# Last stage of a four-layer kernel: all steps turn keys and queries first, and the output rows' product and sum are split around the energies and the masking

## What is computed

```python
# third layer, per head; x is normalized first
q, k, v = silu(x @ Wq), silu(x @ Wk), x @ Wv      # q and k are then multiplied by cos and sin tables
energy = einsum('bhnd,bhmd->bhnm', q, k) * tril
out = einsum('bhnm,bhmd->bhnd', energy, v) @ Wo * sigmoid(x @ G1 @ G2)
x = x + layernorm(layernorm(out) * gamma + beta)
# fourth layer
def step(c, xt):
    ft, it = sigmoid(xt @ wf.T + c @ uf.T + bf), sigmoid(xt @ wi.T + c @ ui.T + bi)
    return ft * c + it * tanh(xt @ wc.T + c @ uc.T + bc)
h = tanh(einsum('tbi,oi->tbo', x, wo) + c_final @ uo.T + bo)
x = x + layernorm(h)
```

## Time and profile before

| | us |
|---|---|
| median of 3 executions | 1415.17 |
| lowest and highest | 1414.31, 1417.53 |
| the profiled execution's own time | 1415.55 |
| its span, first to last instruction | 1413.5 |
| first instruction of step 10's product L1664 | 984.45 |
| first instruction of step 35's product L1664 | 1348.72 |

### The profile page before, as it was taken

The page is one execution under the profiler, slowest core; times in us unless marked ns, Lnnn a source line. Parts: engine busy times, 40 slices in busy tenths (PEclk is TensorE's granted clock), DMA queues, the critical chain, the costliest instruction groups (busy, mean ns, idle before and its releaser), DMA issues. The chain is left out here.

```text
span 1413.5 us, 37117 instructions
## 1 busy us (share of the span) xinstructions
PE 1373.1 (97%) x13346; PEld 1155.1 (82%) x13346; DVE 943.2 (67%) x2208; ACT 695.3 (49%) x1620; POOL 595.6 (42%) x1121
## 2 busy tenths in 40 slices
PE   7999999999999999999999999999999999999995
PEld 6888888788988888888888899777877778787785
DVE  5888888475365555555555532477888888888774
ACT  4666666313444444444444333344555565565553
POOL 3656665233212121212121111646577776776433
PEclk9999999999999999999999999999999999999998
DMA  5433434352111111111111132521211111121000
GB/s 163 126 114 111 132 114 124 119 183 69 42 46 42 42 39 50 39 42 50 43 42 50 38 101 72 173 78 47 61 47 54 61 58 58 46 58 47 10 10 30
DMA packets 88723, 100.02 MB, mean 71 GB/s; under 512 B 12320, under 2 KB 75808, under 8 KB 88544
## 3 DMA queue, kind: packets, MB, share of 16 engines
q1 hardware_dynamic: 80928, 79.04, 18.0%
q0 software_dynamic: 6240, 17.05, 4.2%
q10 hardware_dynamic: 1376, 1.57, 0.3%
HBM read 63.80 MB, written 33.82 MB: 69 GB/s over the span
## 5 line engine op out<-in xcount | busy, mean ns | idle before, releaser
L1022 POOL COPY slot_idx<-source 128x1 int32<-128x1 int32 x58 | 21.3, 367 | 391.2 <-PE wa_Z L1191 376.2
L1058 PE MATMUL wa_P<-ex_xT,lane_w 128*128 128x128 f32 x1440 | 170.7, 275 | 0.0
L1200 PE MATMUL wa_Y<-w,ex_gT 128*128 x720 | 166.2, 380 | 1.6 <-DVE ex_gT L1272 0.9
L1058 PEld LDWEIGHTS wa_P<-ex_xT,lane_w 128*128 128x128 f32 x1440 | 165.7, 192 | 0.2 <-issue 0.2
L1200 PEld LDWEIGHTS wa_Y<-w,ex_gT 128*128 128x128 f32 x720 | 132.1, 190 | 18.9 <-issue 3.2
L1058 PEld LDWEIGHTS wa_qv<-ex_xT,lane_w 128*128 128x128 f32 x720 | 90.6, 191 | 17.9 <-issue 17.4
L1058 PE MATMUL wa_qv<-ex_xT,lane_w 128*128 128x128 f32 x720 | 103.6, 280 | 0.0
L2108 POOL DMA_INDIRECT la_a<-yg,place x64 | 66.8, 1043 | 66.3 <-PE la_E L1702 35.9
L1270 DVE TENSOR_TENSOR ex_gT<-ex_gT,wa_xk 128x256 f32<-128x256 f32 x60 | 25.1, 418 | 103.7 <-ACT ex_gT L1232 103.7
L1230 ACT ACTIVATE ex_gT<-wa_qv 128x256 f32<-128x256 f32 x60 | 23.1, 384 | 138.1 <-PE wa_qv L1058 136.1
L1054 ACT COPY lane_w<-w 128x1408 f32 x60 | 82.0, 1366 | 6.4 <-issue 1.2
(11 more groups left out here) (327 smaller groups left out, 3451.9 us busy)
## 6 DMA issues: line engine op xcount, KB each, us to landing
yg<-ex_yo SPq DMA_DIRECT2D x60, 128.0 KB, 1.7
w<-in_w SPq DMA_DIRECT2D x16, 384.0 KB
w<-in_w SPq DMA_DIRECT2D x16, 352.0 KB, 3.1
w<-in_w SPq DMA_DIRECT2D x16, 320.0 KB, 4.0
wa_xa<-in_x SPq DMA_DIRECT2D x32, 128.0 KB, 2.1
x<-wa_xo SPq DMA_DIRECT2D x32, 128.0 KB, 1.7
xn<-wa_xn SPq DMA_DIRECT2D x32, 128.0 KB, 2.1
xn1T<-wa_x1T SPq DMA_DIRECT2D x32, 128.0 KB, 2.3
```

Source lines behind the costliest of these rows:

```text
L1058: o = e.matmul(out, lane_w[:, i % 2, k, at:at + P], B[i % 2]["xT"][:, k, :], start=(k == 0), stop=(k == KC - 1))
L1200: o = e.matmul(yb[:, 0:C], gT[:, k, :], w2[:, bass.ds(KF * y + k, 1), :], start=(k == 0), stop=(k == KF - 1))
```

## The change

KEYS_FIRST ends at NT + 4 = 36 instead of 10, so steps 10 to 35 also turn queries and keys ahead of the rows, on PE and in ScalarE's copies. For steps up to 35 the output rows' product is taken apart: its first tile's half stays ahead of the energies, its second half goes behind them, ahead of the candidate. VectorE's sum la_h leaves the end of the odd step and follows the four maskings of the next one. ScalarE's tanh moves from near the start of its step to behind la_gt, ahead of the copy la_oT. No instruction is added or removed.

```diff
-        KEYS_FIRST = (4, 10)
+        KEYS_FIRST = (4, NT + 4)
...
-        def rows_product(e, u):
+        def rows_half(e, u, q):
+            for k in range(KC):
+                o = e.matmul(bH[:, q * C:(q + 1) * C], WT[(2 * u + q) % 4][:, k, :], w["wo"][:, k, :],
+                             start=(k == 0), stop=(k == KC - 1))
+            return o
+
+        def rows_free(e, u):
             if u >= 1:
                 e.wait_ge(S["hb"], u)
             else:
                 e.wait_ge(S["b0"], 1)
...
                 for u in pair(s, 11):
                     if s >= NT + 4:
                         carry_product(e, u)
-                    rows_product(e, u)
+                    rows_free(e, u)
+                    rows_half(e, u, 0)
+                    if s >= NT + 4:
+                        rows_half(e, u, 1).then_inc(S["o"], 1)
...
                     o.then_inc(S["en"], 1)
+                for u in pair(s, 11):
+                    if s < NT + 4:
+                        rows_half(e, u, 1).then_inc(S["o"], 1)
...
+                for u in pair(s, 12):
+                    if s - 1 < NT + 4:
+                        output_rows(e, u)
                 if s == 9:
...
                     e.tensor_tensor(p["ucb"][:], carry_bank(u), bo[:], ALU.add).then_inc(S["ucb"], 1)
                     e.wait_ge(S["ucb"], u + 1)
-                    e.wait_ge(S["o"], u + 1)
-                    if u >= 2:
-                        e.wait_ge(S[f"out{u % 2}"], 32 * (u // 2))
-                    e.tensor_tensor(p["h"][:], chunks(bH[:], 2), bc(p["ucb"][:], 1, 2), ALU.add).then_inc(S["hb"], 1)
+                    if s >= NT + 4:
+                        output_rows(e, u)
...
-                for u in pair(s, 12):
-                    if s < DRAIN:
-                        output_tanh(e, u)
...
                     e.activation(d["gt"][:], d["gt"][:], ACT.Copy, scale=0.5, bias=0.5).then_inc(S["gt"], 1)
+                for u in pair(s, 12):
+                    if s < DRAIN:
+                        output_tanh(e, u)
```

More of the change, by code:

```diff
@@ L1541, in rows_product @@
                 e.wait_ge(S["b0"], 1)
[L1542 to L1546, removed]
+        def rows_product(e, u):
+            rows_free(e, u)
+            rows_half(e, u, 0)
+            rows_half(e, u, 1).then_inc(S["o"], 1)
         def carry_product(e, u):
@@ L1792, in sum_stats, with output_rows @@
             norm_stats(e, S, "3", i, B[i % 2]["ln3"], XO[i % 8][:], 3)
+        def output_rows(e, u):
+            p = H[u % 2]
+            e.wait_ge(S["ucb"], u + 1)
+            e.wait_ge(S["o"], u + 1)
+            if u >= 2:
+                e.wait_ge(S[f"out{u % 2}"], 32 * (u // 2))
+            e.tensor_tensor(p["h"][:], chunks(bH[:], 2), bc(p["ucb"][:], 1, 2), ALU.add).then_inc(S["hb"], 1)
         def vector(e):
```

## The result

| | before | after |
|---|---|---|
| median, us | 1414.74 (4 executions) | 1435.85 (4 executions) |
| lowest and highest | 1413.72, 1417.53 | 1435.24, 1435.96 |
| span of the profiled execution | 1413.5 | 1433.2 |
| odd step s = 19 | 14.64 | 16.12 |
| even step s = 18 | 14.48 | 14.97 |

The changed kernel is slower: ratio 1.0142, 95% interval 1.013 to 1.0154, about 20 us where 2.9 were forecast, and outside the forecast range of 1414.0 to 1421.8. (A fourth execution moved the median of before from 1415.17 to 1414.74.) Executions of one and the same kernel mostly fall into two groups some 4 us apart (the kernel before, beside e1 to e4: 1410.9 to 1411.9 and 1415.0 to 1416.2), so the ratios with their intervals are firmer than differences of medians. Nearly the whole difference lies in steps 10 to 35, and mostly in the odd ones.

The account below looks back on a forecast made before the run. PE, busy for 97% of the span, was taken to bound the kernel. Terms of -3.4 (mask wait), +4.3 (even steps) and +2.0 (odd steps) gave +2.9 on the median 1415.17: 1418.1 us, range 1414.0 to 1421.8.

Parts of the forecast that it names:

- part 1: Odd steps 13 to 31: PE's wait for the first masking goes, 0.34 us in each of ten, -3.4 us.
- part 2: Even steps 10 to 34: keys' transposes newly wait for la_y, 0.33 us in each of 13, +4.3 us.
- part 3: Odd steps 13 to 31: keys' transposes wait for late la_y, 0.20 us in each of ten, +2.0 us, from 0 to 6.
- the sum: Whole kernel: -3.4 + 4.3 + 2.0 = +2.9 us on the median, 1418.1 us.
- The first rival: Odd steps: GpSimd's sums stop a second VectorE instruction for 0.42 us each; 1422.3 us, half of that 1420; chance 0.22.
- part 4: Energies' need of la_kT: ScalarE's copy stays covered, margin 0.4 us in odd steps, more in even ones; cost nothing.
- part 5: Candidate's wait for la_ucb: margin grows as PE arrives 0.2 us later; moved tanh delays la_oT by 0.1 at most; nothing.

Follow-up runs that it names:

- e1: Kernel before, with only queries and keys turned ahead of the rows in steps 4 to 35; 1433.9 us, ratio 1.0149 to before.
- e4: Changed kernel with GpSimd's addition of la_h and la_xo shrunk to one column of each tile; 1421.6 us, ratio 1.0052 to before.
- e2: Changed kernel with rows first again from step 10; split product, moved sum and tanh stay; median 1414.0 us, ratio 1.0005 to before.
- e8: Split product, rows first from step 10, plus the even steps' gate products with inputs ahead of the wait for la_c; 1409.9 us, ratio 0.9970 to before.
- e3: Changed kernel with rows first again in even steps from 10 on, queries and keys first in odd steps; ratio 1.0002 to before.
- e11: Changed kernel with three useless 128x1 GpSimd instructions added at the end of even steps; 1420.1 us, ratio 1.0029 to before.
- e9: Changed kernel with one useless 128x1 GpSimd instruction added at the end of even steps; 1430.4 us, ratio 1.0126 to before.
- e5: Kernel before with one more keys' transpose on PE in even steps 10 to 34, 0.11 us each; 1417.3 us.
- e6: Kernel before with two more keys' transposes on PE in even steps 10 to 34, 0.22 us per step; 1429.2 us.

## Why the prediction was wrong

**The mask wait goes (part 1): right.** None of the ten is left, and odd steps of e2 take 14.31 us, 0.33 less than before. The wait also cost the next even step some 0.07 us (e8), which the 0.34 left out. What the 0.17 us beyond the shown idle time are, which the prediction calls the restart of the pipeline, no run separates; only the loss itself is measured.

**Keys first in even steps (part 2): right in place and size.** In the even step of the changed kernel whose window stands above, the keys' transposes start 0.77 us behind the queries' instead of 0.43:

```profile
1116.19 0.60 PE L1745 MATMUL la_E<-consts,la_qr 128*128 128x128 f32 x4
1116.96 0.63 PE L1753 MATMUL la_E<-consts,la_kr 128*128 128x128 f32 x4 [0.17 <-DVE la_y L1920]
```

**Keys first in odd steps (part 3): wrong, by the size of one term, and this is the step that failed.** It put the shift of 0.33 us and the collisions into the sum as 0.20 us per odd step, with 0.6 as the upper bound. The changed kernel loses 16.12 - 14.31 = 1.81 us there: 0.19 by the order alone (e3), 0.20 by the moved la_x and la_xo and 1.41 by the addition into la_h (e4). The first rival, that GpSimd's sums stretch more of VectorE, named the mechanism and priced it at 0.42 more per step; that was too little by a factor of four, and for the two sums that it had in view twice too much, as it overlooked that la_xo already held a normalization of la_h. Two things were missed. First, the bound took GpSimd to move by 0.33 us, as far as PE moves it. It moves by 0.6, because la_ln_ve passes in front of la_qr and is no longer held. In the kernel before, it stood 0.13 us behind. Second, only la_x and la_xo were looked at. A third, longer piece, the addition into la_h, started 0.75 us behind the second la_ym before. After the change it comes 0.36 us earlier and la_ym 0.21 later, so it starts 0.18 behind it, and la_ym was the one that was held, for 1.4 us. The upper bound should have been made of all of GpSimd's large instructions ahead of la_y, about 0.42 + 1.4 us per odd step; the range would then have reached to 1436. Both gaps stand in the trace of the kernel before, in odd step 19 (VectorE and GpSimd), and were not weighed:

```profile
1118.23 0.69 DVE L1827 TENSOR_TENSOR la_qr<-la_qks,la_cs 128x512 f32<-128x512 f32 x1 [1.48 <-ACT la_qks L2042]
1118.36 0.64 POOL L1340 TENSOR_SCALAR la_ln_ve<-la_ln_mv 128x1 f32<-128x1 f32 x1
...
1123.60 0.48 DVE L1885 SCALAR_TENSOR_TENSOR la_ym<-la_a,weight,la_ym 128x256 f32<-128x256 f32 x1
...
1124.35 1.42 POOL L2122 TENSOR_TENSOR la_h<-la_h,la_xo 128x256 f32<-128x256 f32 x2
```

On the mutual exclusion the Trainium skill ("SBUF — State Buffer", section "Who interferes with whom") says of the port pair that VectorE and GpSimd share that "it's an exclusive lock". The runs bear that out in kind. The addition into la_h added 1.4 us to la_ym, its own whole length, and even a 128x1 instruction was held for 0.53 us by la_qr.

The same section says that issue order decides who blocks. By the recorded starts that held for la_ln_ve, to 0.01 us, and for la_fc, which started 0.14 us ahead of la_x and kept its 0.42 us, but not for la_ym, which started 0.18 us ahead and lost. Recorded starts may be too coarse for this: held VectorE instructions end some 0.29 us behind the one that held them, so of the 0.48 us of a free la_ym about 0.19 would lie ahead of the point at which it can be stopped (an estimate from these rows). With that, 0.18 us is a tie. No run settles it.

**Cover for ScalarE's copies (part 4): right.** PE has no wait for la_kT in steps 10 to 35.

**The candidate, and the rest (part 5): incomplete.** The candidate never waits for la_ucb. But nothing was said of what PE's earlier start does in the next even step. There it waits for la_c, 0.17 us in the changed kernel and 0.36 in e2. That is why the even steps grew by 5.7 us where 4.3 were forecast.

**The sum.** Where the order of la_ln_ve and la_qr is kept, as in e11, the change costs 0.29% (0.13 to 0.45) or 4.1 us, and the stretch from step 10 to step 35 takes 368.94 us, 4.7 more than before. The sum had 2.9; its even steps take 14.99 us where 14.81 were forecast, and 0.18 us in each of ten explains the gap. The mechanism of the sum holds on one side of an edge, and the change itself pushed the kernel across it.

## What to carry to other kernels

A steady pattern of steps is a fixed alignment of engines, and a small delay of one moves it. Before pricing a wait on the bounding engine, list which instructions of two engines that exclude each other stand next to each other in time, with the gap in us, and ask which order flips: here two instructions that started 0.13 us apart stood between a kernel at 1414 us and one at 1430. A wait moved onto a new producer makes every delay of that producer count, so its range must hold all that can stretch the producer, not only what stretches it now. And where a removed wait doesn't shorten the step, look for the next wait on the same partner: once the gate's input products covered it, the two edits together were worth 0.3%.

## What was unexpected in the hardware

- A GpSimd instruction on one number per partition is held by a VectorE instruction of two SBUF inputs that started 0.01 us earlier, for 0.53 us; started 0.07 us before it (e9) it takes its 0.21 us. When it is held it ends 0.07 to 0.09 us behind the other, wherever it started (before, e5, e11).
- Work added to GpSimd, 36 small instructions, brought the changed kernel from 1.0128 to 1.0029 of the kernel before, while 26 transposes added on TensorE (e6), 2.9 us of work, made the stretch from step 10 to step 35 of the kernel before 17.7 us longer.
- Independent 128x1 instructions in a row cost GpSimd 0.17 to 0.18 us each (e11, e9), where la_ln_rs starts 0.30 us behind the la_ln_ve that it needs.
